# Hyperbolic attention stage: head-by-head storage, two chunks per ScalarE instruction, sums and squares dealt out anew

## What is computed

```
q_h, k_h, v_h = exp_map(q), exp_map(k), exp_map(v)         # points of the Poincare ball
diff = xns - 2 * einsum('bhsd,bhtd->bhst', q_h, k_h) + yns
arg  = maximum(1 + 2*c*diff / maximum((1-c*xns)*(1-c*yns), EPS), 1 + EPS)
dist = 1/sqrt(c) * arccosh(arg)
weights = softmax(-beta * dist - bias, axis=-1)
out  = einsum('bhst,bhtd->bhsd', weights, log_map(v_h))
return concat(log_map(exp_map(out))) @ W_o.T
```

## Time and profile before

| | |
|---|---|
| median of 3 runs | 7286.41 us (7283.5 to 7287.61) |
| the profiled execution | 7294.11 us, its span 7292.3 us |
| mean granted TensorE clock | 0.762 of full speed |
| VectorE busy | 4717.3 us, 65% |
| ScalarE busy | 4687.7 us, 64% |
| TensorE busy with matmuls | 4547.1 us, 62% |
| GpSimd busy | 1329.5 us, 18% |
| DMA sums: share of the 16 DMA engines | 36.6% |

### The profile page before, as it was taken

One profiled execution on the slowest core, in us unless ns is written; L12 is line 12 of the kernel. 1 busy time (PEld: TensorE's weight loads), 2 busy tenths in 40 slices (PEclk: granted clock), 3 DMA queues, 4 the chain that ended last, 5 costly groups with the idle time before them and its releaser, 6 DMA issues. The chain is left out here.

```text
span 7292.3 us, 78431 instructions
## 1 busy us (share of the span) xinstructions
PE 4547.1 (62%) x23556; PEld 2300.8 (32%) x23556; DVE 4717.3 (65%) x6664; ACT 4687.7 (64%) x4434; POOL 1329.5 (18%) x1152
## 2 busy tenths in 40 slices
PE   7999999899999974343444434445344454445456
PEld 5666666666666662000000000002100010001004
DVE  5555555555555554776776767774767787768684
ACT  4544555455445542677787777886488888888893
POOL 0000000000000000332333323231233333333320
PEclk9999999999999986566666656666566666666666
DMA  1000000000000002777776777875468686878681
GB/s 32 6 6 6 9 6 6 5 6 6 7 6 9 2 3 58 126 145 131 137 136 124 150 135 131 150 145 122 104 132 165 140 159 133 165 139 159 133 174 58
DMA packets 330626, 631.71 MB, mean 87 GB/s; under 512 B 167814, under 2 KB 263752, under 8 KB 264264
## 3 DMA queue, kind: packets, MB, share of 16 engines
q0 software_dynamic: 73728, 536.90, 36.6%
q1 hardware_dynamic: 256584, 90.74, 7.1%
HBM read 69.50 MB, written 21.23 MB: 12 GB/s over the span
## 5 line engine op out<-in xcount | busy, mean ns | idle before, releaser
L1436 PE MATMUL psum<-b_qT,b_kT 126*128 126x512 bf16 x2048 | 894.4, 538 | 1855.4 <-DVE b_tiles L1195 1852.3
L1195 DVE SCALAR_TENSOR_TENSOR b_tiles<-b_ra_rep,b_cap,psum 128x1024 f32<-128x1024 f32 x1024 | 1261.1, 1271 | 1063.7 <-DMA b_tiles<-b_tiles 535.9
L1436 PEld LDWEIGHTS psum<-b_qT,b_kT 126*128 126x128 bf16 x2048 | 140.6, 109 | 2771.4 <-DVE b_tiles L1195 2715.7
L1329 ACT ACTIVATE b_tiles<-b_tiles 128x2048 f32<-128x2048 f32 x320 | 598.3, 1904 | 539.4 <-DVE b_tiles L907 449.1
L567 DVE CUSTOM_DVE_ANT_0 a_srow<-psum,a_bias 128x1024 f32<-128x1024 f32 (+7 forms) x768 | 679.2, 909 | 146.7 <-PE psum L703 74.1
L1202 DVE TENSOR_SCALAR b_tiles<-b_tiles 128x2048 f32<-128x2048 f32 x512 | 752.3, 1469 | 5.5
L638 ACT ACTIVATE a_srow<-a_srow,a_nmax 128x640 f32<-128x640 f32 (+15 forms) x512 | 615.8, 1203 | 121.2 <-DVE a_nmax L573 90.7
L1339 ACT ACTIVATE b_tiles<-b_tiles,b_sc 128x2048 f32<-128x2048 f32 x320 | 659.3, 2079 | 0.0
L1448 PE MATMUL psum<-b_tiles,b_v_aug 128*32 128x512 f32 x2560 | 548.8, 947 | 132.2 <-ACT b_tiles L1339 131.9
L1334 ACT ACTIVATE b_tiles<-b_tiles 128x2048 f32<-128x2048 f32 x320 | 599.8, 1898 | 0.9
L725 PE MATMUL psum<-ident,a_srow 128*128 128x128 f32 x4352 | 577.7, 277 | 16.7 <-DVE a_pT L484 11.5
(11 more groups left out here) (218 smaller groups left out, 7310.2 us busy)
## 6 DMA issues: line engine op xcount, KB each, us to landing
b_tiles<-b_tiles POOLq DMA_DIRECT2D x320, 1024.0 KB, 14.9
X<-b_tiles POOLq DMA_DIRECT2D x192, 1024.0 KB, 16.1
b_ra_rep<-ra_scratch SPq DMA_DIRECT2D x32, 1024.0 KB, 27.5
a_wqk<-in_wqk_dram SPq DMA_DIRECT2D x64, 128.0 KB, 2.8
x_scratch<-X SPq DMA_DIRECT2D x8, 1024.0 KB, 10.9
kv_scratch<-b_tiles SPq DMA_DIRECT2D x4, 2048.0 KB, 9.1
X<-x_scratch SPq DMA_DIRECT2D x8, 1024.0 KB, 10.6
X<-in_x_dram SPq DMA_DIRECT2D x4, 1024.0 KB, 9.5
```

The source lines that it names most:

```text
L1195: nc.vector.scalar_tensor_tensor(out=a[:, s * HALF:(s + 1) * HALF], in0=ra_rep[:, j, s * HALF:(s + 1) * HALF], scalar=cap[:, j, k:k + 1], ...
L1329: nc.scalar.activation(y, y, ACT.Sqrt, bias=-1.0).then_inc(S["root_done"], 1)
L1436: last = nc.tensor.matmul(half_ps(s)[:, i * BANK:(i + 1) * BANK], kT[:, j, k * P:(k + 1) * P], qT[:, j, cs], start=True, stop=True)
```

## The change

All of it is in `stage_attn_b`.

- `A_SLOTS` becomes one ring of seven slots and `Y_SLOTS` one of ten, counted through all heads.
- ScalarE's `root`, `log` and `weight` take two neighbouring slots in one instruction of 4096 elements a partition. The exponential of a pair follows its logarithm at once.
- `SQUARES`: of each four chunks VectorE squares the first two, GpSimd the last two. `SUMS`: the first three of each four sums are DMAs, the fourth is an addition by VectorE (`own_sum`), placed five chunks later (`SUM_LAG`), ahead of `argument`.
- `prep` is cut into `prepare` parts 0, 1 and 2, done two heads ahead, each behind another batch's squares. k and v are loaded into `k_raw` and `v_raw` and copied from there by GpSimd (`take_v` for v).
- `tok`, `arr`, the k and v scratch and the `ra` scratch hold one head's values together, so that a head's piece per partition is 1 KB for k and v and 8 KB for `ra_rep`.
- The loops over batch elements and heads are written out instead of `Fori`, and the `passed` semaphore is gone.

```diff
-SQUARES = "DDPD" * 4
+SQUARES = "DDPP" * 4
+SUMS = "MMMD" * 4
+SUM_LAG = 5
-A_SLOTS = [6, 7, 8, 9, 14, 2] * 2 + [6, 7, 8, 9, 14] * 4
-Y_SLOTS = [10, 11, 12, 13, 15, 16, 17, 18, 3, 4, 5] * 2 + [10, 11, 12, 13, 15, 16, 17, 18, 3, 4]
+A_SLOTS = [6, 7, 8, 9, 14, 2, 5]
+Y_SLOTS = [10, 11, 12, 13, 15, 16, 17, 18, 3, 4]
...
-        def y_slot(k, j):
-            s = Y_SLOTS[j * NCHK + k]
-            return tiles[:, s, :] if s < 15 else x_ring[:, s - 15, :]
+        def y_slot(h, k, n=1):
+            s = Y_SLOTS[(h * NCHK + k) % Y_BACK]
+            slots = tiles[:, s:s + n, :] if s < 15 else x_ring[:, s - 15:s - 15 + n, :]
+            return slots.rearrange("p s n -> p (s n)")
...
             for k in range(n * BATCHED, (n + 1) * BATCHED):
-                eng.wait_ge(S["root_done"], g * NCHK + k + 1)
-                eng.sem_inc(S["passed"], 1)
-                engine.dma_start(y_slot(k, j), a_slot(k, j), accum_op=ALU.add).then_inc(S[f"sum{k % 8}"], 16)
+                if SUMS[k] != "M":
+                    continue
+                eng.wait_ge(S["root_done"], pairs_to(b * HB + h, k))
+                engine.dma_start(y_slot(h, k), a_slot(h, k), accum_op=ALU.add).then_inc(S[f"sum{k % 8}"], 16)
...
-                    src = ra_scratch[bass.ds(b, 1)].rearrange("a (t h) k -> (a h) t k", h=HB)[bass.ds(h, 1)]
-                    sp.dma_start(ra_rep[:, j, :].rearrange("p (t k) -> p t k", k=P), src.to_broadcast([P, TB, P])
-                                 ).then_inc(S[f"ra_loaded{j}"], 16)
+                    src = ra_scratch[bass.ds(b, 1)].rearrange("a (h t) k -> (a h) (t k)", h=HB)[bass.ds(h, 1)]
+                    sp.dma_start(ra_rep[:, h % 2, :], src.to_broadcast([P, SEQ])).then_inc(S[f"ra_loaded{h % 2}"], 16)
...
-                for n in range(NCHK // BATCHED):
-                    squares(pool, nc.gpsimd, b * HB + HB - 1, n, 1)
-                    sums(pool, nc.gpsimd, b * HB + HB - 1, n, 1)
+                for part in range(3):
+                    prepare(pool, nc.gpsimd, b, 1, part)
+                squares(pool, nc.gpsimd, b, 0, 0)
+                last = NCHK // BATCHED - 1
+                for h in range(HB):
+                    for n in range(last + 1):
+                        sums(pool, nc.gpsimd, b, h, n)
+                        if n < last:
+                            squares(pool, nc.gpsimd, b, h, n + 1)
+                        elif h + 1 < HB:
+                            squares(pool, nc.gpsimd, b, h + 1, 0)
+                        if n == 2 and h + 1 < HB:
+                            take_v(pool, nc.gpsimd, b, h + 1)
+                        if n > 0 and h + 2 < HB:
+                            prepare(pool, nc.gpsimd, b, h + 2, n - 1)
...
+                def own_sum(n):
+                    h, k = n // NCHK, n % NCHK
+                    if SUMS[k] == "D":
+                        dve.wait_ge(S["root_done"], pairs_to(b * HB + h, k))
+                        y = y_slot(h, k)
+                        nc.vector.tensor_tensor(y, y, a_slot(h, k), ALU.add).then_inc(S["sum_dve"], 1)
...
                     for k in range(NCHK):
-                        argument(g, k, j, first)
+                        if h or k >= SUM_LAG:
+                            own_sum(h * NCHK + k - SUM_LAG)
+                        argument(h, k)
...
-                def root(g, k, j):
-                    act.wait_ge(S["sq_" + SQUARES[k]], squared(g, k) + 1)
-                    y = y_slot(k, j)
+                def root(h, k):
+                    g = b * HB + h
+                    for i in range(k, k + 2):
+                        act.wait_ge(S["sq_" + SQUARES[i]], squared(g, i) + 1)
+                    y = y_slot(h, k, 2)
                     nc.scalar.activation(y, y, ACT.Sqrt, bias=-1.0).then_inc(S["root_done"], 1)
...
-                    ks = range(n * BATCHED, (n + 1) * BATCHED)
-                    for k in ks:
-                        log(g, k, j)
-                        if k > ks[0]:
-                            weight(g, k - 1, j)
-                    weight(g, ks[-1], j)
+                    for k in range(n * BATCHED, (n + 1) * BATCHED, 2):
+                        log(k // NCHK, k % NCHK)
+                        weight(k // NCHK, k % NCHK)
...
-                    pe.wait_ge(S["w_done"], g * NCHK + k + 1)
+                def product(h, k):
+
+                    g, j = b * HB + h, h % 2
+                    pe.wait_ge(S["w_done"], pairs_to(g, k))
```

More of the change, by code:

```diff
@@ L988, in _ @@
             sp.dma_start(sc[:, LOGC:BETA + 1], scalars.to_broadcast([P, 2])).then_inc(S["scal_loaded"], 16)
[L989 removed]
+            for b in range(BATCH):
                 sp.wait_ge(S["x_added"], b * TB)
@@ L1046, in _ @@
+                load_ra(0)
+                for h in range(1, HB):
+                    load_k(h)
+                    load_v(h)
+                    load_ra(h)
                 sp.wait_ge(S["av_done"], av((b + 1) * HB * NCHK))
@@ L1061, in _ @@
             pool.wait_ge(S["zeroed"], 2)
-            with pool.Fori(0, BATCH) as b:
+            for b in range(BATCH):
                 pool.wait_ge(S["v_ready"], b + 1)
@@ L1233, in _ @@
                 dve.wait_ge(S["grp_copied"], b * HB * 4 + 4)
-                def head(h, j, first, last):
-                    nonlocal g_par
-                    g = b * HB + h
+                g_par = 0
+                dve.wait_ge(S["x_saved"], (b + 1) * 64)
+                dve.wait_ge(S["kv_saved"], (b + 1) * 32)
+                for h in range(HB):
+                    g, j = b * HB + h, h % 2
                     dve.wait_ge(S[f"ra_loaded{j}"], (g - j) * 8 + 16)
@@ L1301, in _ @@
             nc.scalar.activation(col(T + 9), col(T + 7), ACT.Ln).then_inc(S["scal"], 1)
-            with act.Fori(0, BATCH) as b:
+            for b in range(BATCH):
                 act.wait_ge(S["x_added"], b * TB)
@@ L1383, in _ @@
             pe.sem_inc(S["av_done"], AHEAD)
-            with pe.Fori(0, BATCH) as b:
+            for b in range(BATCH):
                 for q in range(TB // 4 + 1):
```

331 lines of the change are left out of this document (151 added, 180 removed).

## The result

The kernel after takes **6533.89 us** (median of 4 runs, 6533.58 to 6534.62) against 7287.01 (4 runs, 7283.5 to 7289.26): a ratio of 0.8967, 95% interval 0.8951 to 0.8983. I had said 6594, with 6440 to 6840 around it. The profiled execution is one of 6534.62 us.

The account below looks back on a forecast made before the run. The prediction took the two chunk loops to be bound by waits between engines, chiefly late DMA sums. Savings of 655 us in the loops, 30 and 7 made 692: 7286.4 - 692 = 6594 us, range 6440 to 6840.

Parts of the forecast that it names:

- (1) The load: `ra_rep` read in 8 KB runs lands in 8 us (bounds 5 and 11); waits at loop starts shrink, -30 us.
- The third rival: Sums stay late because the load stays slow or sums bunch on GpSimd: 125 us a head, about 7150 us; chance 0.05.
- (2) Preparation: GpSimd's preparation cut into three parts, the longest about 9 us; still delays one batch's sums, 1.7 us a head.
- (3) Seven slots: `A_SLOTS` is 7 where it was 5 or 6, so `argument` waits for the sum seven chunks back; no size given.
- (4) Three DMA sums a batch: Three DMA sums a batch instead of four, so a batch's last sum lands 5.2 us sooner.
- (5) Pairs: ScalarE works on two chunks per instruction: batch 24.5 us, head 98.0, a gain of only 2.7 a head.
- (6) Own sums and GpSimd's squares: VectorE trades four squares a head for four sums, GpSimd squares eight; costs VectorE 0 to 4.8 us a head.
- The chain that I wrote down: From exponentials through product, scores, `argument`, clamp, own sum and GpSimd's square to the second root pair; slack 0.3 us.
- The second rival: VectorE and GpSimd exclude each other and become the bound: 112 us a head, 6812 us; chance 0.22.
- The fourth rival: It gets slower because written-out code must be fetched: 132 us a head, 7336 us; chance 0.03.
- the term of 7 us: With loops written out, VectorE's issue idle time at the turn of the batch loop goes: -7 us.
- the four delays: Group transposes, `out_copy` with `out_scale`, preparation, and load with small work add 6 us to 98, giving 104 a head.

Follow-up runs that it names:

- e1: Kernel after with only the DRAM layout of the ra array as before, so `ra_rep` loads in 512 B pieces: 6978.55 us.
- e2: Kernel before with only the ra array stored head by head and `ra_rep` loaded in 8 KB runs: 6802.9 us.
- e3: Kernel after with the three preparation parts together again, behind the squares of a head's last batch: 6740.75 us.
- e12: Kernel after with one chunk per ScalarE instruction, all sums as DMAs, GpSimd squaring one chunk of four, still seven `a` slots: 6487.30 us.
- e4: Kernel after with five slots in `A_SLOTS` instead of seven: 7360.84 us.
- e11: Kernel after with one chunk per ScalarE instruction, all sums as DMAs, GpSimd squaring one chunk of four, and five `a` slots: 6780.14 us.
- e5: Kernel after with all four sums of a batch as DMAs, none on VectorE: 6410.51 us.
- e8: Kernel after with VectorE's own sum placed behind `argument` of the same chunk instead of ahead of it: 6415.18 us.
- e7: Kernel after with one chunk per ScalarE instruction instead of pairs: 6491.23 us.
- e9: Kernel after with products eleven chunks behind the scores instead of ten (`V_LAG` 11): 6516.97 us.
- e10: Kernel after with `V_LAG` 11, all sums as DMAs, GpSimd squaring the second and fourth chunks, both logarithms before both exponentials: 6509.17 us.

## Why the prediction was right, point by point

**The bound.** Right. Waits for sums were the stalls, and the late sums had two causes, the load (e1, e2) and the preparation (e3).

**(1) The load.** The mechanism was right, the term mis-sized: 4.8 us where I took 8, below my lower bound of 5. I had bounded it by rows of transfers that read each byte once, and this one spreads a single 8 KB row. What runs beside it counts as well: medians of the same load are 6.4 us in e2, 7.8 in e12 and 10.3 in e3. The waits at the loop starts gave 38 us, not 30. The third rival, that it stays slow, is out; the Trainium skill, "DMA: Bandwidth & Descriptors", § Specifications, calls 512 B enough for full rate, and here 512 B against 8 KB pieces is 24.6 against 4.8 us for the same 1024 KB (e1 and the kernel after). For this load the measurement decides.

**(2) Preparation.** Right: 207 us when put back. Of the wait of 1.7 us that I left for it, ScalarE shows at most 0.7, in the batch of 25.2, where `argument` waits for a sum that went out 13.9 us after the batch's table load (I had 13.7) and landed about when I said.

**(3) Seven slots.** The prediction listed them and gave them no price. That was its gap, though not a wrong number: they carry 827 us with pairs (e4) and 293 without (e11, e12). Had the ring stayed at five, the change would have lost time, and none of my rivals said so.

**(4) Three DMA sums a batch.** I said that the last one lands 5.2 us sooner. From issue to landing the longest sum takes 17.6 us instead of 22.6 (the kernel after against e5), the median one 11.5 instead of 14.4. So that is right, and nothing needed it: the kernel with four is faster.

**(5) Pairs.** The batch of 24.5 us and the head of 98.0 were right to 0.2 and 0.3 us (e5, e8; root pairs of 3.62 where I had 3.61). In the kernel after only one batch of four has that length, and e7 shows that there pairs cost 43 us on balance.

**(6) Own sums and GpSimd's squares.** The chain that I wrote down ends where the trace shows it, in the second pair of roots behind GpSimd's square. I took both squares and own sums for equal in cost and saw only their lengths. I put GpSimd's square "behind" the own sum and didn't say that it could stand first. It is this order that costs: e8 turns it round and gets 119 us, nearly all that lies between the kernel after and the floor. More clamps of 2.4 us, which I expected, did not come: the longest is 2.35 us, and their mean is 1471 ns as against 1469 before. VectorE is busy 94.5 us a head (1512.47/16), not 96.7, and the 2.6 us over the 91.9 of before are those of the own sums, four a head with a mean of 2.99 us instead of 2.28.

**The second rival**, exclusion, has a true mechanism and a wrong price. I gave each of two squares a batch 2 us of VectorE's time, 16 a head. The squares grew by 0.74 us each, 5.9 a head, and VectorE's work by 2.6, and only what falls into the chain counts. The trace therefore bears out the exclusion but not the 112 us that I drew from it.

**The fourth rival**, fetching of code, did not show. The idle time of VectorE put down to issue at the turn of the batch is gone, as the term of 7 us had it. Ahead of TensorE's weight loads in the stage some 690 us of such time stood before and 720 stand after, and with all batches of e5 at 24.5 or 24.6 us none of it is on the chain.

**The sum.** Of the loops I was 52 us over. Start to first `out_copy` 179 instead of 185 (12 in two loops), thirteen heads at 102.3 to 102.4 instead of 104 (43), the last head 98.5 instead of 100 (3), the end 63.3 instead of 60 (-7). Outside the loops I was 16 under, 53 against 37. Together the saving is 67.5 us larger by the profiled executions (759.5 against 692); the profiled execution of before was 7 above its median and that of after 1, so 60 remain, 6594 against 6534.

The term that was mis-sized is the four delays: 6 us a head forecast, 102.3 - 98.0 = 4.3 measured. One by one they fit less well than their sum.

- `out_copy` and `out_scale`: their batch has 3.1 us, where I had 2 to 3. But VectorE is late in it also by the 3.03 us of an own sum that stood behind a square, which I hadn't put there.
- Preparation: 0.7 instead of 1.7, and 0.5 of it is what the batch of 25.0 has without it.
- Scores: those 0.5 in the batch of 25.0 are no delay of my list. Two products and the scores behind them take 3.06 us, where I added up 2.2 from the earlier trace rows.
- Group transposes: I had 1 to 1.5. `argument` is some 1 us later for them (4.00 against 3.06), and the batch still has 24.5, since the square goes ahead of the own sum there.
- The load and small work, for which I had 1, show in no batch.

That these errors nearly cancel is luck.

## What to carry to other kernels

Look first at what lands late together, then at the queue that issued it, then at how many slots must cover the time from write to release: here 491, 23 to 207 and 293 us. Of the new dealing on top of them, pairs and GpSimd's second square brought 77 us, and VectorE's own sums, as placed, lost 123. Where two engines exclude each other for whole large instructions, the order of two instructions in one queue decides: put the one that the other engine may run beside (here `argument`) behind the release of its work. Before a product or a sum is moved by a chunk, count every ring that it frees (e9). Such edits don't add up: e5 and e8 each win some 120 us by one edit, and e10, with e5's and three more, wins 25.
